# A scan in four-step blocks: how many groups of state are added over PSUM in each step, and when the next block's decays are made

## The chip, the cores and the metric

The kernel runs on one core of a Trainium2 chip. The metric is the time of one execution on the device in microseconds, as the median of several runs. A profiled execution of the same program gives the trace that the text reads; its engines are called PE (TensorE), DVE (VectorE), ACT (ScalarE), POOL (GpSimd) and SP (SyncE, which only issues DMAs here).

## The reference, cut to what matters

A small vision tower of two layers runs over 64 images of 37 tokens and 256 features. The token layer embeds patches; layer 0 has a state-space block ("attn") and a mixture of experts; layer 1 has attention and another mixture. The change lies in the scan of the state-space block:

```python
def _L0_attn_ref(up_x, ...):
    ...
    delta = jax.nn.softplus(x @ W_delta + b_delta)
    Bm = x @ W_B + b_B
    Cm = x @ W_C + b_C
    A = -jnp.exp(A_log)
    dA = jnp.exp(delta[..., None] * A)
    dBx = delta[..., None] * Bm[:, :, None, :] * x[..., None]
    def step(h, inputs):
        dA_t, dBx_t, C_t = inputs
        h = dA_t * h + dBx_t
        y_t = jnp.einsum('bdn,bn->bd', h, C_t)
        return (h, y_t)
```

There are 37 steps. The state h of one step has 64 images x 128 channels x 64 values, in float32.

## The kernel before, in words

**Layout.** Two images share the 128 partitions (64 values of n each), so the state of a step is 32 pairs x 128 channels = 4096 columns. It lies in one of eight slots of SBUF, `slot[slot_of(t)]`. The 4096 columns are four groups (GROUPS, m = 0 to 3) of 1024, and each group is two halves of 512, one PSUM bank each.

**Blocks.** Steps 1 to 36 form nine blocks of four (BLK = 4). The decays dA of a whole block are made ahead, into the four slots in which that block's states will then be formed (the decay is multiplied in place). They are made in 32 "quads" (QUADS, four channels each): `make_quad` (L1181) has PE multiply into one of three PSUM banks, `exp_quad` (L1654, its activation on L1659) has ACT take the exponential into the slots. The three banks (DECAY_BANKS, 0 to 2) are a ring that quads and the turned rows of y share; `RING_AT` gives each its place, the semaphore `made` counts the banks that PE filled, `taken` those that ACT emptied. `quads_made(t, m)` says which quads of the next block are made behind group m of step t, on PE and ACT alike: 32 quads spread evenly from group 3 of the block's first step on, so 2, 10, 10 and 10 in its four steps. ACT's first quad of a block waits until the first step of the running block has consumed the slots. DVE's first decay of a block waits for all of them (L2010).

**A step on DVE.** A group is treated in one of two ways. In the first (groups 0 and 2), DVE multiplies the slot's decay by the state before (`decay_state`, L2014), PE forms the injection dBx as two products of 512 columns in the banks 3 and 4 (`inject`, its matmuls on L1188 and L1195 by `make_quad` and `inject_rows`), and DVE adds it (`add_injected`, L2033; L2030 in step 0). In the second (groups 1 and 3, "grown"), DVE writes decay times state straight into the banks 5 and 6, half by half (`seed_state`, L2022), PE adds the injection on top of it in the bank (`grow`, matmuls on L1195), and ACT copies the sum to the slot (`copy_grown`, L1686). There is one pair of banks for each way, so each seed half waits until the copy before it has emptied its bank, and each injection until the add before it is done. The semaphores are `multed`, `injected` and `added` for the first way, `seeded`, `grown` and `copied` for the second; every wait is for a count.

**Reading.** `read_state` (L1228) multiplies half of a step's state (groups 0 and 1, or 2 and 3) by windows of C that POOL sets (L1044), eight matmuls into bank 7. ACT evicts the bank every other step (`evict_rows`, L1668), PE turns the rows (`turn_y`, L1239) into a ring bank and ACT copies y out (`copy_y`, L1678).

**The order is written out by hand.** Each engine takes its own list strictly in order. PE in step t: inject(0), the read of groups 2 and 3 of the step before, the quads behind group 0; grow(1), quads; inject(2), the read of groups 0 and 1, quads; grow(3), in odd steps turn_y, quads. ACT: quads of group 0; in odd steps evict_rows; the copies of group 1, quads; quads of group 2; the copies of group 3, in odd steps copy_y, quads. DVE: decay 0, seeds 1, add 0, decay 2, seeds 3, add 2. SP loads the injection's operands three steps ahead (`load_inject`, L891 and L892) when `injected` and `grown` tell that a buffer is free, and loads a block's delta rows when `made` allows.

Of the kernel before, what the change touches and what calls it, by code (L numbers as in the profile page):

```python
# [13 lines left out]
NI, L = 64, 37  # L14
# [86 lines left out]
def build(nc, small, dense, patches, w_lin, a_rows, up0, dn0, w1, w2, b1, b2, gates_dram, slots,  # L101
          rows_dram, delta_dram, late_rows, late_delta, h_dram, gate_dram, out):
    with ExitStack() as ctx:
# [641 lines left out]
        def quads_made(t, m):  # L745


            b = block_of(t) + 1
            if t == 0 or b >= NBLK:
                return []  # L750
            u = (t - BLK * (b - 1) - 1) * GROUPS + m - 3
            if u < 0:
                return []
            n = BLK * GROUPS - 3
            return [(b, k) for k in range(QUADS * u // n, QUADS * (u + 1) // n)]

# [25 lines left out]
        def _(sp):  # L782
# [98 lines left out]
            def load_inject(t):  # L881

                if t >= INJ:
                    sp.wait_ge(injected, 2 * (t - INJ + 1))
                    sp.wait_ge(grown, 4 * (t - INJ + 1))
                n = t % INJ
                dx_rows, b_rows = [rows_dram[w, t % 2, :, :, t // 2 * P:t // 2 * P + P].rearrange(
                    "(m p) k d -> (p k) m d", m=GROUPS) for w in range(2)]
                for x in range(8):
                    rows = slice(16 * x, 16 * x + 16)  # L890
                    sp.dma_start(dx_in[n][rows, :, x % 4, :], dx_rows[rows]).then_inc(inject_in[n], 16)  # L891
                sp.dma_start(b_in[n], b_rows).then_inc(inject_in[n], 16)  # L892
# [47 lines left out]
            sp.dma_start(hF, h_dram).then_inc(kept_back, 16)  # L940
            sp.wait_ge(multed, 2 * (L - BLK))
            sp.wait_ge(seeded, 4 * (L - BLK))
            sp.wait_ge(read_ps, 2 * (L - BLK))
# [5 lines left out]
            sp.wait_ge(read_ps, 2 * L)  # L949
            sp.wait_ge(added, 2 * L)  # L950
            sp.dma_start(up0s, up0).then_inc(ffn0_in, 16)
# [30 lines left out]
        def _(pool):  # L982
# [66 lines left out]

            pool.wait_ge(injected, 2 * L)  # L1050
            pool.wait_ge(grown, 4 * L)
            nc.gpsimd.memset(xn[:, :, T:TP], 0.0).then_inc(zeros_set, 1)
# [42 lines left out]
        def _(pe):  # L1095
# [103 lines left out]
            def inject(t, m):  # L1199

                if m == 0:
                    pe.wait_ge(inject_in[t % INJ], 16 * 9 * (t // INJ + 1))
                pe.wait_ge(added, 2 * t + m // 2)
                inject_rows(t, m, 0, INJ_BANK, True)
                inject_rows(t, m, 1, INJ_BANK + 1, True).then_inc(injected, 1)

            def grow(t, m):

                for half in range(2):
                    if t >= 1:  # L1210
                        pe.wait_ge(seeded, 4 * (t - 1) + m - 1 + half + 1)
                    elif m == 3:
                        pe.wait_ge(copied, half + 1)
                    inject_rows(t, m, half, GROW_BANK + half, t == 0).then_inc(grown, 1)

            def read_state(t, r):

                yb, tp = y_block(t)
                first = r == 0 and (tp == 0 or t == 0)
                pe.wait_ge(added, 2 * t + r + 1)  # L1220
                pe.wait_ge(copied, 4 * t + 2 * r + 2)
                pe.wait_ge(window, 4 * t + 4)
# [38 lines left out]
            for t in range(L + 1):  # L1261
                for m in range(GROUPS):
                    if 1 <= t < L and m % 2 == 0:
                        inject(t, m)
                    if 1 <= t < L and m % 2 == 1:
                        grow(t, m)
# [304 lines left out]
        def _(act):  # L1571
# [109 lines left out]
            def copy_grown(t, m):  # L1681

                for half in range(2):
                    act.wait_ge(grown, 4 * t + m - 1 + half + 1)
# [13 lines left out]
            for t in range(L + 1):  # L1698
                for m in range(GROUPS):
                    if m == 1 and t % 2 == 1:  # L1700
                        evict_rows(t // 2)
                    if 1 <= t < L and m % 2 == 1:
                        copy_grown(t, m)
                    if t < L and m == 3 and t % 2 == 1:
                        copy_y(t // 2)
                    for b, k in quads_made(t, m) if t < L else []:
                        if k == 0:
                            act.wait_ge(read_ps, 2 * (BLK * (b - 1) + 1))
                            act.wait_ge(multed, 2 * (BLK * (b - 1) + 1))
                            act.wait_ge(seeded, 4 * (BLK * (b - 1) + 1))  # L1710
# [142 lines left out]
        def _(dve):  # L1853
# [151 lines left out]
            GW = GP * P  # L2005

            def decay_state(t, m):

                if m == 0 and (t - 1) % BLK == 0:
                    dve.wait_ge(taken, block_taken(block_of(t)))  # L2010
                dve.wait_ge(added, 2 * (t - 1) + m // 2 + 1)
                now, before = slot[slot_of(t)], slot[slot_of(t - 1)]
# [3 lines left out]
            def seed_state(t, m):  # L2016

                now, before = slot[slot_of(t)], slot[slot_of(t - 1)]
                for half in range(2):
                    hs = slice((2 * m + half) * 512, (2 * m + half + 1) * 512)  # L2020
                    dve.wait_ge(copied, 4 * (t - 1) + m - 1 + 2 + half + 1)
                    nc.vector.tensor_tensor(ps[:, GROW_BANK + half, :], now[:, hs], before[:, hs],  # L2022
                                            ALU.mult).then_inc(seeded, 1)

            def add_injected(t, m):

                now = slot[slot_of(t)][:, m * GW:(m + 1) * GW].rearrange("p (b n) -> p b n", b=2)
                dve.wait_ge(injected, 2 * t + m // 2 + 1)
                if t == 0:
                    nc.vector.tensor_copy(now, ps[:, INJ_BANK:INJ_BANK + 2, :]).then_inc(added, 1)  # L2030
                else:
                    dve.wait_ge(multed, 2 * (t - 1) + m // 2 + 1)
# [376 lines left out]
```

## Time and profile before

| what | us |
|---|---|
| median of 3 runs | 1099.65 (1097.55 to 1106.23) |
| the profiled execution | 1094.59 |
| its span in the trace | 1092.7 |
| first decay of step 1 to the last read of the scan | 152.22 to 449.75 of that span |
| the rest: ahead of the scan / behind it | 152.2 / 643.0 |

Times in the rows are microseconds from the span's start, and mean durations are nanoseconds where marked. The brackets at the end of a timeline row give how long the engine was idle before it and whose instruction released it. PEclk is the granted clock of TensorE as a share of full speed: 1.0 is 2.4 GHz and 0.5 is 1.2 GHz. "L" numbers are lines of the kernel before.

### The profile page before, as it was taken

The page shows a single profiled execution, that of the slowest core. Times are in us where ns is not written, and L with a number is a line of the kernel's source. Part 1 is how long each engine was busy: PE and PEld are TensorE (multiplying, and loading weights), DVE is VectorE, ACT ScalarE, POOL GpSimd, SP SyncE. Part 2 cuts the span into 40 slices and gives each one's busy share as a digit, 9 for nine tenths or more (in the row PEclk, how much of TensorE's full clock was granted, in tenths as well). Part 3 has the DMA queues.
Part 4 walks back from the last instruction along what each step waited for, and adds up shares of the span by engine and source line. Part 5 has one row for each costly group of instructions (what it writes and reads, how often), then busy time and mean ns, then how long its engine had stood idle before and what let it go on. Part 6 is the DMA issues. An engine that isn't in the chain of part 4 may idle for free.

```text
span 1092.7 us, 17549 instructions
## 1 busy us (share of the span) xinstructions
PE 921.2 (84%) x5861; PEld 582.3 (53%) x5862; DVE 669.3 (61%) x1176; ACT 503.3 (46%) x1019; POOL 294.6 (27%) x357
## 2 busy tenths in 40 slices
PE   8997487877777777799999999999999996469996
PEld 6773443333323322346677777666667664336664
DVE  2533987988888988754554455477777773213332
ACT  1226577877779776343122222335444432323332
POOL 4922922333333310000000000074445410612222
PEclk9999768988999889999999999999999996579999
DMA  6282769453221212850411111000000002322220
GB/s 247 98 285 98 229 206 313 118 131 71 51 54 34 54 30 70 357 233 7 130 45 45 44 46 43 0 1 1 1 1 0 1 1 115 153 90 86 83 85 26
DMA packets 96258, 100.66 MB, mean 92 GB/s; under 512 B 64318, under 2 KB 81471, under 8 KB 94528
## 3 DMA queue, kind: packets, MB, share of 16 engines
q1 hardware_dynamic: 93456, 92.50, 26.7%
q0 software_dynamic: 2736, 7.30, 1.8%
q8 instruction: 39, 0.64, 0.2%
q14 instruction: 27, 0.22, 0.1%
HBM read 73.10 MB, written 39.18 MB: 103 GB/s over the span
## 4 chain that ended last, share of the span: by engine, by line
PE 64%; ACT 11%; DVE 10%; issue 7%; SPq 3%; DMA 3%; POOL 0%; ACTq 0%; DVEq 0%; POOLq 0%
PE ps L556 9%; PE ps L618 8%; PE ps L1228 6%; ACT mem L1659 5%; PE ps L1109 4%; PE ps L1518 4%; PE ps L1534 4%; PE ps L1431 3%; PE ps L1365 3%; PE ps L1188 3%; SPq L891 2%; PE ps L1387 2%; PE ps L1195 2%; ACT mem L1686 2%; DVE mem L2014 2%
## 5 line engine op out<-in xcount | busy, mean ns | idle before, releaser
L1066 POOL TENSOR_TENSOR mem<-mem,sm 128x296 f32<-128x296 f32 x128 | 87.2, 716 | 346.5 <-ACT mem L1754 306.4
L1659 ACT ACTIVATE mem<-ps 128x512 f32<-128x512 f32 x288 | 154.2, 629 | 24.0 <-PE ps L1188 12.9
L1044 POOL TENSOR_SCALAR mem<-mem,sm 128x16 f32<-128x16 f32 x148 | 105.4, 735 | 170.8 <-PE ps L1228 170.8
L556 PE MATMUL ps<-mem 128*128 (+1 forms) x384 | 110.2, 416 | 0.6 <-DVE mem L529 0.6
L1188 PE MATMUL ps<-mem 64*128 64x128 bf16 x1140 | 91.9, 232 | 20.6 <-ACT mem L1659 11.3
L1228 PE MATMUL ps<-mem 128*32 128x512 f32 x592 | 89.1, 675 | 22.3 <-issue 13.2
L1686 ACT ACTIVATE mem<-ps 128x512 f32<-128x512 f32 x148 | 82.3, 607 | 51.2 <-PE ps L1195 51.1
L1188 PEld LDWEIGHTS ps<-mem 64*128 64x128 bf16 x1140 | 56.4, 100 | 90.1 <-ACT mem L1659 69.4
L2014 DVE TENSOR_TENSOR mem<-mem 128x1024 f32<-128x1024 f32 x72 | 87.8, 1219 | 26.7 <-ACT mem L1659 26.7
L1195 PE MATMUL ps<-mem 64*128 64x512 bf16 x296 | 76.3, 424 | 31.5 <-DVE ps L2022 21.6
L2022 DVE TENSOR_TENSOR ps<-mem 128x512 f32<-128x512 f32 x144 | 93.6, 695 | 14.9 <-ACT mem L1686 14.3
L618 PE MATMUL ps<-mem 128*128 128x296 f32 x352 | 99.9, 413 | 2.5 <-DVE mem L682 2.5
L642 ACT ACTIVATE mem<-ps 128x296 f32<-128x296 f32 x88 | 36.8, 418 | 135.0 <-PE ps L556 135.0
L2033 DVE TENSOR_TENSOR mem<-mem,ps 128x1024 f32<-128x1024 f32 x72 | 87.4, 1214 | 2.1 <-PE ps L1195 1.6
L556 PEld LDWEIGHTS ps<-mem 128*128 128x128 f32 x384 | 73.1, 191 | 25.1 <-issue 2.1
L618 PEld LDWEIGHTS ps<-mem 128*128 128x128 f32 x352 | 66.6, 190 | 24.2 <-DVE mem L682 3.9
L682 DVE TENSOR_TENSOR mem<-mem 128x296 f32<-128x296 f32 x88 | 41.1, 467 | 36.5 <-ACT mem L642 34.3
L1195 PEld LDWEIGHTS ps<-mem 64*128 64x128 bf16 x296 | 21.2, 97 | 71.3 <-DVE ps L2022 54.7
L676 DVE TENSOR_TENSOR mem<-mem 128x296 f32<-128x296 f32 x64 | 29.9, 467 | 45.3 <-ACT mem L642 39.4
L1518 PE MATMUL ps<-mem 128*128 x104 | 51.1, 615 | 7.7 <-issue 7.1
L1109 PE MATMUL ps<-mem 128*128 128x288 f32 x192 | 50.7, 417 | 5.1 <-DMA mem<-in_patches 5.1
L463 DVE TENSOR_TENSOR mem<-mem 128x592 f32<-128x592 f32 (+1 forms) x32 | 26.2, 817 | 46.7 <-ACT mem L436 46.7
(240 smaller groups left out, 1573.1 us busy)
## 6 DMA issues: line engine op xcount, KB each, us to landing
mem<-gates SPq DMA_DIRECT2D x7, 1184.0 KB, 6.0
mem<-in_w SPq DMA_DIRECT2D x2, 4096.0 KB, 16.3
slots<-mem SPq DMA_DIRECT2D x1, 6682.0 KB, 23.6
mem<-slots SPq DMA_DIRECT2D x26, 257.0 KB, 2.7
mem<-in_patches SPq DMA_DIRECT2D x7, 864.0 KB, 4.7
mem<-factor_rows SPq DMA_DIRECT2D x296, 16.0 KB, 1.8
mem<-factor_rows SPq DMA_DIRECT2D x37, 128.0 KB, 2.3
mem<-delta_rows SPq DMA_DIRECT2D x9, 512.0 KB, 4.5
```

Of the source, the lines that this page charges most:

```text
L556: mm = nc.tensor.matmul(ps[:, bank, 0:CH], w[:, k, row0:row0 + P], xn[:, k, cols], start=(k == 0), stop=(k == HALVES - 1))
L618: mm = nc.tensor.matmul(ps[:, 1 + 2 * cj + m, 0:CH], dn_w[:, j - 2, m * P:(m + 1) * P], hid2[:, b, :], start=(j == 2 and n == nt), stop=(j ...
L1044: nc.gpsimd.tensor_scalar(c_win4[:, t % SLOTS * 2 + r, :, w0:w0 + 8].rearrange("p j (x i) -> p j x i", i=2)[:, :, :, i], c_all[:, r * 16:r ...
L1109: mm = nc.tensor.matmul(ps[:, 2 * j + m, 0:IC * NP], wl[:, f, m * P:(m + 1) * P], xin[:, j, f, :], start=(f == 0), stop=(f == FK - 1))
L1188: mm = nc.tensor.matmul(ps[:, ring_bank(at_), e * BT:(e + 1) * BT], a_stat[64 * r:64 * r + 64, g, e, :], delta_in[b % 2][64 * r:64 * r + 6 ...
L1195: return nc.tensor.matmul(ps[:, bank, :], b_in[t % INJ][rows, m, :], dx_in[t % INJ][rows, m, :, :].rearrange("p x n -> p (x n)"), start=st ...
L1228: mm = nc.tensor.matmul(ps[32 * j:32 * j + 32, Y_BANK, :], c_win[:, win:win + 32], slot[slot_of(t)][:, quad * 512:(quad + 1) * 512], start ...
L1518: mm = nc.tensor.matmul(ps[:, 2 + j, 0:HID1], slot_xT[j][:, k, :], w1s[:, k, ds(e * HID1, HID1)], start=(k == 0), stop=(k == 1))
L1659: nc.scalar.activation(decay_slots[b % 2][:, :, 4 * k:4 * k + 4], ps[:, ring_bank(at_), :].rearrange("p (e t) -> p t e", e=4), ACT.Exp).th ...
L1686: nc.scalar.activation(slot[slot_of(t)][:, quad * 512:(quad + 1) * 512], ps[:, GROW_BANK + half, :], ACT.Copy).then_inc(copied, 1)
L2014: nc.vector.tensor_tensor(now[:, gs], now[:, gs], before[:, gs], ALU.mult).then_inc(multed, 1)
L2022: nc.vector.tensor_tensor(ps[:, GROW_BANK + half, :], now[:, hs], before[:, hs], ALU.mult).then_inc(seeded, 1)
```

## The change

Which groups are grown now depends on the step. In step 0 they are 1 and 3 as before. In the first step of each block, and in all of the last four steps (33 to 36), they are 1, 2 and 3. In the second step of a block they are 1 and 3, in the third and fourth only group 1. Over a block that is 3, 2, 1 and 1 in place of 2, 2, 2 and 2. The next block's quads are spread anew: one behind group 3 of the first step, then 8, 11 and 12 in the second to fourth step, evenly over their groups. All waits that counted two groups a step by arithmetic now look their counts up in two tables, `ADDED_AT` and `GROWN_AT`, or count with `added_to` and `grown_to`. A seed now waits for the state of the step before in so many words (`wait_state`), as a decay does. PE's, ACT's and DVE's loops keep their order over the groups; each group is simply injected or grown as the table says.

```diff
-            u = (t - BLK * (b - 1) - 1) * GROUPS + m - 3
-            if u < 0:
-                return []
-            n = BLK * GROUPS - 3
-            return [(b, k) for k in range(QUADS * u // n, QUADS * (u + 1) // n)]
+            at_ = t - BLK * (b - 1) - 1
+            first, n = ((0, 1), (1, 8), (9, 11), (20, 12))[at_]
+            if at_ == 0:
+                return [(b, 0)] if m == 3 else []
+            return [(b, k) for k in range(first + n * m // GROUPS, first + n * (m + 1) // GROUPS)]
+
+        def grown_groups(t):
+
+            if t == 0:
+                return (1, 3)
+            if (t - 1) % BLK == 0 or t >= L - BLK:
+                return (1, 2, 3)
+            return (1, 3) if (t - 1) % BLK == 1 else (1,)
+
+        ADDED_AT, GROWN_AT = {}, {}
+        for t in range(L):
+            for m in range(GROUPS):
+                if m in grown_groups(t):
+                    GROWN_AT[t, m] = len(GROWN_AT)
+                else:
+                    ADDED_AT[t, m] = len(ADDED_AT)
+
+        def added_to(t, m=GROUPS - 1):
+
+            return len([g for g in ADDED_AT if g <= (t, m)])
+
+        def grown_to(t, m=GROUPS - 1):
+
+            return len([g for g in GROWN_AT if g <= (t, m)])
...
-                    sp.wait_ge(injected, 2 * (t - INJ + 1))
-                    sp.wait_ge(grown, 4 * (t - INJ + 1))
+                    sp.wait_ge(injected, added_to(t - INJ))
+                    sp.wait_ge(grown, 2 * grown_to(t - INJ))
...
-                pe.wait_ge(added, 2 * t + m // 2)
+                pe.wait_ge(added, ADDED_AT[t, m])
...
-                        pe.wait_ge(seeded, 4 * (t - 1) + m - 1 + half + 1)
+                        pe.wait_ge(seeded, 2 * GROWN_AT[t, m] - 4 + half + 1)
...
-                pe.wait_ge(added, 2 * t + r + 1)
-                pe.wait_ge(copied, 4 * t + 2 * r + 2)
+                pe.wait_ge(added, added_to(t, 2 * r + 1))
+                pe.wait_ge(copied, 2 * grown_to(t, 2 * r + 1))
...
-                    if 1 <= t < L and m % 2 == 0:
+                    if 1 <= t < L and (t, m) in ADDED_AT:
                         inject(t, m)
-                    if 1 <= t < L and m % 2 == 1:
+                    if 1 <= t < L and (t, m) in GROWN_AT:
                         grow(t, m)
...
+            def wait_state(t, m):
+
+                if m in grown_groups(t):
+                    dve.wait_ge(copied, 2 * GROWN_AT[t, m] + 2)
+                else:
+                    dve.wait_ge(added, ADDED_AT[t, m] + 1)
...
             for t in range(L):
-                for m in range(0, GROUPS, 2):
-                    if t >= 1:
-                        decay_state(t, m)
-                        seed_state(t, m + 1)
-                    add_injected(t, m)
+                for m in range(GROUPS):
+                    by_pe = grown_groups(t)
+                    if m not in by_pe:
+                        if t >= 1:
+                            decay_state(t, m)
+                        if t >= 1 and m + 1 in by_pe:
+                            seed_state(t, m + 1)
+                        add_injected(t, m)
+                    elif t >= 1 and m - 1 in by_pe:
+                        seed_state(t, m)
```

So DVE's order in a step with three grown groups is decay 0, seeds 1, add 0, seeds 2, seeds 3, and with one: decay 0, seeds 1, add 0, decay 2, add 2, decay 3, add 3. The same replacement of counts is made in ACT's, POOL's and SP's other waits.

## Rows read from the trace of the kernel before

**Rows 1.** The page: span, busy time and share of each engine
```profile
span 1092.7 us, 17549 instructions
...
PE 921.2 (84%) x5861; PEld 582.3 (53%) x5862; DVE 669.3 (61%) x1176; ACT 503.3 (46%) x1019; POOL 294.6 (27%) x357
```
**Rows 2.** Windows by block: stretch, length, busy by engine, PEclk, DMA share, GB/s
```profile
152.22:188.76 36.54, 29.05 (x258) 11.53 (x250) 28.43 (x32) 26.78 (x55) 8.72 (x17) 0.86 0.96 306
188.76:221.66 32.90, 25.14 (x240) 10.56 (x240) 28.42 (x33) 26.06 (x53) 12.06 (x17) 0.90 0.48 125
221.66:255.09 33.43, 25.51 (x240) 11.00 (x240) 28.51 (x32) 26.04 (x53) 12.04 (x17) 0.90 0.49 126
...
288.82:321.20 32.38, 24.20 (x240) 10.03 (x240) 28.31 (x33) 26.05 (x53) 9.99 (x17) 0.95 0.23 51
...
421.84:449.75 27.91, 18.78 (x103) 5.26 (x103) 27.85 (x32) 11.03 (x20) 0.20 (x1) 0.94 0.58 219
```
**Rows 3.** Waits between 222 and 421 us (total, times, longest)
```profile
ACT mem L1686 <- PE ps L1195: 30.1, 14, 3.2
DVE mem L2014 <- ACT mem L1659: 18.8, 6, 3.1
...
DVE ps L2022 <- ACT mem L1686: 9.2, 17, 0.7
```
**Rows 4.** Timeline from the head of the block of steps 9 to 12
```profile
221.66 1.23 DVE L2014 TENSOR_TENSOR mem<-mem 128x1024 f32<-128x1024 f32 x1 [3.13 <-ACT mem L1659]
222.80 1.31 DVE L2022 TENSOR_TENSOR ps<-mem 128x512 f32<-128x512 f32 x2
...
223.55 0.43 PE L1195 MATMUL ps<-mem 64*128 64x512 bf16 x1 [2.23 <-DVE ps L2022]
224.01 0.60 ACT L1686 ACTIVATE mem<-ps 128x512 f32<-128x512 f32 x1 [1.90 <-PE ps L1195]
224.02 1.21 DVE L2033 TENSOR_TENSOR mem<-mem,ps 128x1024 f32<-128x1024 f32 x1
...
225.15 1.21 DVE L2014 TENSOR_TENSOR mem<-mem 128x1024 f32<-128x1024 f32 x1
...
225.83 1.93 PE L1228 MATMUL ps<-mem 128*32 128x512 f32 x8
226.29 1.29 DVE L2022 TENSOR_TENSOR ps<-mem 128x512 f32<-128x512 f32 x2
...
227.69 0.61 PE L1195 MATMUL ps<-mem 64*128 64x512 bf16 x2
...
228.23 2.08 PE L1239 MATMUL ps<-sm,mem 128*128 128x128 f32 x8
...
230.53 0.14 PEld L1195 LDWEIGHTS ps<-mem 64*128 64x128 bf16 x2
...
233.34 1.09 ACT L1686 ACTIVATE mem<-ps 128x512 f32<-128x512 f32 x2
```
**Rows 5.** Timeline in other steps: turn, y copy, exponentials, products and a read
```profile
210.32 1.16 PE L1239 MATMUL ps<-sm,mem 128*128 128x128 f32 x8
...
212.12 0.35 ACT L1678 ACTIVATE mem<-ps 128x128 f32<-128x128 f32 x1
212.29 1.62 ACT L1659 ACTIVATE mem<-ps 128x512 f32<-128x512 f32 x3
...
290.71 0.39 PE L1195 MATMUL ps<-mem 64*128 64x512 bf16 x1 [2.23 <-DVE ps L2022]
...
297.05 1.06 PE L1228 MATMUL ps<-mem 128*32 128x512 f32 x8
```
**Rows 6.** Timeline of the first block: two waits that a DMA ended
```profile
162.35 2.06 ACT L1659 ACTIVATE mem<-ps 128x512 f32<-128x512 f32 x4 [2.16 <-DMA late_rows<-mem]
...
178.90 0.39 PE L1195 MATMUL ps<-mem 64*128 64x512 bf16 x2 [0.69 <-DMA mem<-factor_rows]
```
**Rows 7.** Timeline: the last read of the scan
```profile
449.75 1.07 PE L1228 MATMUL ps<-mem 128*32 128x512 f32 x8 [0.73 <-DVE mem L2033]
```

More of the change, by code:

```diff
@@ L940, in _ @@
             sp.dma_start(hF, h_dram).then_inc(kept_back, 16)
-            sp.wait_ge(multed, 2 * (L - BLK))
-            sp.wait_ge(seeded, 4 * (L - BLK))
+            sp.wait_ge(multed, added_to(L - BLK) - 2)
+            sp.wait_ge(seeded, 2 * grown_to(L - BLK) - 4)
             sp.wait_ge(read_ps, 2 * (L - BLK))
@@ L949, in _ @@
             sp.wait_ge(read_ps, 2 * L)
-            sp.wait_ge(added, 2 * L)
+            sp.wait_ge(added, added_to(L - 1))
             sp.dma_start(up0s, up0).then_inc(ffn0_in, 16)
@@ L1048, in _ @@
                             S("c_half")[:, i:i + 1], None, ALU.mult).then_inc(window, 1)
-            pool.wait_ge(injected, 2 * L)
-            pool.wait_ge(grown, 4 * L)
+            pool.wait_ge(injected, added_to(L - 1))
+            pool.wait_ge(grown, 2 * grown_to(L - 1))
             nc.gpsimd.memset(xn[:, :, T:TP], 0.0).then_inc(zeros_set, 1)
@@ L1683, in copy_grown @@
                 for half in range(2):
-                    act.wait_ge(grown, 4 * t + m - 1 + half + 1)
+                    act.wait_ge(grown, 2 * GROWN_AT[t, m] + half + 1)
                     quad = 2 * m + half
@@ L1701, in _ @@
                         evict_rows(t // 2)
-                    if 1 <= t < L and m % 2 == 1:
+                    if 1 <= t < L and (t, m) in GROWN_AT:
                         copy_grown(t, m)
@@ L1708, in _ @@
                             act.wait_ge(read_ps, 2 * (BLK * (b - 1) + 1))
-                            act.wait_ge(multed, 2 * (BLK * (b - 1) + 1))
-                            act.wait_ge(seeded, 4 * (BLK * (b - 1) + 1))
+                            act.wait_ge(multed, added_to(BLK * (b - 1) + 1) - 2)
+                            act.wait_ge(seeded, 2 * grown_to(BLK * (b - 1) + 1) - 4)
                             if b == 1:
@@ L2010, in decay_state @@
                     dve.wait_ge(taken, block_taken(block_of(t)))
-                dve.wait_ge(added, 2 * (t - 1) + m // 2 + 1)
+                wait_state(t - 1, m)
                 now, before = slot[slot_of(t)], slot[slot_of(t - 1)]
@@ L2016, in seed_state @@
             def seed_state(t, m):
+                wait_state(t - 1, m)
                 now, before = slot[slot_of(t)], slot[slot_of(t - 1)]
@@ L2020, in seed_state @@
                     hs = slice((2 * m + half) * 512, (2 * m + half + 1) * 512)
-                    dve.wait_ge(copied, 4 * (t - 1) + m - 1 + 2 + half + 1)
+                    dve.wait_ge(copied, 2 * GROWN_AT[t, m] - 2 + half + 1)
                     nc.vector.tensor_tensor(ps[:, GROW_BANK + half, :], now[:, hs], before[:, hs],
@@ L2027, in add_injected @@
                 now = slot[slot_of(t)][:, m * GW:(m + 1) * GW].rearrange("p (b n) -> p b n", b=2)
-                dve.wait_ge(injected, 2 * t + m // 2 + 1)
+                dve.wait_ge(injected, ADDED_AT[t, m] + 1)
                 if t == 0:
@@ L2031, in add_injected @@
                 else:
-                    dve.wait_ge(multed, 2 * (t - 1) + m // 2 + 1)
+                    dve.wait_ge(multed, ADDED_AT[t, m] - 2 + 1)
                     nc.vector.tensor_tensor(now, now, ps[:, INJ_BANK:INJ_BANK + 2, :], ALU.add).then_inc(added, 1)
             for t in range(L):
-                for m in range(0, GROUPS, 2):
-                    if t >= 1:
-                        decay_state(t, m)
-                        seed_state(t, m + 1)
-                    add_injected(t, m)
+                for m in range(GROUPS):
[8 more added lines that the diff above has]
+                        seed_state(t, m)
             dve.wait_ge(kept_back, 16 * 4)
```

## The prediction

> **What bounds the kernel now.** The page comes first: a span of 1092.7 us, TensorE (PE) busy for 84% of it, VectorE (DVE) for 61%, ScalarE (ACT) for 46% [rows 1]. Those shares average over stages, and the edit lies in one of them, so the view that counts is the table of windows with one row for each block of four steps [rows 2]. There DVE is busy 28.4 to 28.5 us of some 33 and ACT 26.05. Neither is full, and both have nearly as much to do as the block is long. From T = 188.76 (first decay of the block of steps 5 to 8) to T = 421.84 lie seven blocks, 33.30 us each. The first takes 36.54 with the DMA rings at 0.96, and the last, which makes no decays, 27.91. The waits tell what the missing 5 us are: DVE's largest is for the exponentials, 3.1 us ahead of each block (18.8 us in six blocks), then 9.2 us for ACT's copies ahead of seeds. ACT in turn waits 30.1 us for the products of grown groups, 14 times [rows 3]. So a block begins with ACT waiting for DVE and ends with DVE waiting for ACT: a load that is uneven in time, which is what the edit addresses.
>
> **Unit costs.** In one block [rows 4]: decay at 221.66, its seed pair at 222.80, the add at 224.02, the next decay at 225.15. So DVE issues a decay every 1.13 us, a seed pair takes 1.21, an add 1.13. A group with decay and add costs 2.26, a grown one 1.21; a step of two and two 6.94. ACT issues a copy or exponential every 0.49 (a pair takes 1.09, one 0.60); after a y copy it is free in 0.17 (212.12 to 212.29) [rows 4, 5]. A seed half runs 0.69, its product starts 0.06 later and takes 0.39 to 0.43, the copy starts at once and takes 0.60: 1.85 us from the seed's start until its bank is free.
>
> **The change, counted.** Grown groups go from 2,2,2,2 to 3,2,1,1 in the four steps of a block. DVE: 5.89 + 6.94 + 7.99 + 7.99 = 28.8 us for 27.8 before. ACT: 14 copies for 16, 1.0 us less. Decays still take 32 exponentials, now 1, 8, 11, 12 for 2, 10, 10, 10. The products number the same on PE. The renumbered waits on SP and POOL ask for the same events, so their queues aren't moved past anything: 0. The added wait ahead of a seed asks for the state of the step before, which the bank wait behind it or DVE's own order had already: 0; only seeds and adds are queued behind it. Totals hardly change, so the time depends on the chain. I follow it in two parts, cut at c, the end of the copies of group 1 in the block's second step.
>
> *From T to c.* Before: 221.66 to 233.34 + 1.09 = 234.43, 12.77 us [rows 4]. Its chain was seed of group 3 at T+4.63, read of the state (1.93), product at T+6.03, the turn of y (2.08), the first decays, injection at T+8.87, read, decays, product, copy [rows 4]. Now group 3's seed needs the banks that group 2 has just taken: group 1 seeded at 1.13, add 2.35, group 2 seeded at 3.49, its copies end at 5.26 and 5.87, group 3 seeded at 5.31 and 5.92, DVE free at 6.52 (0.42 earlier than 6.94, not the counted 1.05). On PE the read sits between the products of groups 2 and 3. With a read at 1.06 and a turn at 1.16 [rows 5]: read 5.1 to 6.1, product 6.1 and 6.67, turn from 6.95, quad 8.04, injection 8.25, read 8.6, two quads 9.6 to 10.05, their exponentials until 10.88, copies until 11.97. The read and the turn are at their slow lengths in most blocks of before, though, and these now lie in series behind a product that comes later: 0.9 more for a slow read and 0.9 for a slow turn. Slow read alone: c = 12.4 to 12.9; both: 13.3 to 13.7. I take 12.75, nearest to the row of before, 12.77.
>
> *From c to the next T.* Before: 255.09 - 234.43 = 20.66 [rows 2, 4], in which ACT has 28 exponentials, 10 copies, an eviction and a y copy: 38 x 0.49 + 0.66 = 19.3, and 1.4 of gaps. Now 29 exponentials, 6 copies and the same two: 35 x 0.49 + 0.66 = 17.8. The gaps grow, since with two quads made a turn ACT runs out while PE reads: after the copies it is busy 0.87, the next quad comes 1.30 after them. That is 0.43 twice in the second step, 0.44 ahead of the turn in the third, and 0.54 behind a read at the start of the fourth: 1.85 in all, so 19.7. DVE in the same part: 0.65 of waiting for the third injection of the third step, and at the end it waits 1.1 instead of 3.1, since group 3 of the last step is no longer a copy in front of the last exponentials.
>
> Block: 12.75 + 19.7 = 32.45 for 33.43, 0.97 less. Seven of them: -6.8 us. The first block has waits for DMA in it (0.69 at an injection, 2.16 at an exponential [rows 6]) that a faster step would only lengthen: -0.5, between -1.5 and 0.
>
> *The last four steps* have three grown groups each and no decays. Before, DVE paces them, 27.91 us from T to the last read [rows 2, 7]. The count promises 4 x 1.05 = 4.2 less. But the round trip of 1.85 through one pair of banks three times a step, with the read between, and two turns of y, brings the last read to T+28.1 by the same hand working, since that read now waits for a copy (0.5 behind the seed's product) and no longer for an add. With a slow clock there, 29. I take +0.5; ends -4.2 and +1.1.
>
> **Sum.** -6.8 - 0.5 + 0.5 = -6.8 us. The profiled execution took 1094.59 (1.9 around its span of 1092.7) and becomes 1087.8. The median of the runs shown lies 5.1 higher, 1099.65, and takes the same difference: 1092.9, say 1093.
>
> **The clock.** The blocks' granted clock is 0.90 (0.95 in one), that is 6.7 us (3.2 us) of each at 1.2 GHz [rows 2]. It shows after PE had stood idle for 2.23 us and then in short gaps: products of 0.61 in place of 0.39, reads of 1.93 in place of 1.06 [rows 4, 5]. The block with 0.95 is the shortest, 32.38. In the changed kernel the idle stretch at the block's head is about as poor in work: between T+0.4 and T+5.1 only the four products of groups 1 and 2, in gaps of 1.5, 0.2 and 1.3 us.
>
> The Trainium skill (TensorE: Matmul & The Clock Gate, "A second HAM failure mode: psum-queue depth-cycling") says that a kernel which cycles PSUM in each iteration leaves micro-idles between groups of matmuls that make the clock swing between its two levels. The trace agrees for the idle of 2.23 us; no row shows three groups in a row through one bank pair, and by this rule they would be what the last rival below prices.
>
> **Rivals.**
> (A) The forecast, 1093, chance 0.46; its own range 1089 to 1096.
> (B) The clock stays high at most block heads, as it does in the last steps of before. For: the 3.13 us wait that opened the gap is gone. Against: the gaps just listed. T to c is 12.0, so 1.6 to 1.75 less for each of seven blocks, -1.5 in the first: about -13, 1086. Chance 0.18.
> (C) DVE's count alone decides, the gaps of ACT close up: 6.52 + 6.94 + 7.99 + 7.99 + 0.6 for the last exponentials = 30.0 a block, 3.3 less: -23, 1077. For: ACT's counted work, 48 x 0.49 and two y copies, is 24 us. Against: quads come in threes through three banks, and ACT had such gaps before too. Chance 0.10.
> (D) The gain of the second part is lost in the first: c at 13.3 to 13.7 in most blocks, within 2 us of no change, 1099. For: the late product of group 3. Chance 0.16.
> (E) Slower. Place: the first step of each block, where three seeds go through one pair of banks. If the clock falls later than before and still is low at the turn of y and at the read behind it, each doubles: injection at T+10.5, read until 12.4, c at 15.0, so 2.2 more in the first part against 0.97 less in the second: +1.25 in eight blocks, +2 in the last steps, +12: 1112. It decides from c = T+13.75 on. Chance 0.10.
> That the edit doesn't do what it says is no case: orders and counts follow from the code.
>
> **From these to the numbers.** A measurement here can tell about 1% (11 us) from no change. Faster by over 1% (under 1088.7): C, nearly all of B, a little of A: 0.28. Slower by over 1%: 0.08, most of E. Within 1%: 0.64. For 8 in 10 the range leaves out C, most of E: 1081 to 1103.
>
> **What would show it.** Right: windows of the seven blocks at 32.4 on average; DVE's wait for exponentials at each head 0.9 to 1.5 in place of 3.1; seed pairs of groups 2 and 3 that take 1.3, 0.6 apart; c at T+12 to 13; exponentials ahead of c three, not four; the last read 28 to 29 after the last T. Wrong: a wait at the head over 2 us; c to T' over 20.3; an injection that DVE waits for in every step (PE's order would be the bound); last steps under 26. The forecast falls if the granted clock of the scan leaves 0.90 by more than 0.04.

## The result, and the profile after

The changed kernel is slower: a median of 1113.73 us (1111.8 to 1116.13, 4 runs) against 1098.75 (4 runs), a ratio of 1.0119 with a 95% interval of 1.0089 to 1.015. Forecast were 1093, in a range from 1081 to 1103.

The profiled execution has a span of 1114.2 us, 21.5 more than before. First the windows by block, the same view as [rows 2] (stretch, length, busy time by engine, PEclk, DMA share, GB/s), and the parts ahead of and behind the scan:

```profile
0.00:155.89 155.89, 126.62 (x648) 90.91 (x649) 78.08 (x114) 67.32 (x126) 81.43 (x67) 0.87 0.53 182
...
155.89:191.88 35.99, 29.57 (x258) 11.61 (x250) 29.84 (x32) 26.35 (x52) 8.28 (x16) 0.84 0.99 304
191.88:226.35 34.47, 26.46 (x244) 11.24 (x240) 29.76 (x32) 25.63 (x50) 9.77 (x16) 0.90 0.48 127
...
363.31:397.45 34.14, 26.35 (x244) 11.04 (x240) 29.75 (x32) 25.63 (x50) 9.76 (x16) 0.90 0.22 47
...
431.59:464.86 33.27, 23.64 (x107) 6.86 (x104) 24.65 (x32) 15.36 (x28) 0.21 (x1) 0.74 0.49 185
464.86:1114.20 649.34, 582.41 (x3181) 406.74 (x3181) 333.28 (x774) 215.32 (x456) 131.20 (x173) 0.93 0.18 60
```

and the two outer parts of the kernel before:

```profile
0.00:152.22 152.22, 122.35 (x648) 88.25 (x649) 80.06 (x115) 67.28 (x126) 81.19 (x67) 0.89 0.54 186
...
449.75:1092.70 642.95, 573.89 (x3181) 401.74 (x3181) 333.72 (x774) 215.86 (x456) 131.24 (x173) 0.94 0.18 61
```

The 21.5 us split into +3.7 ahead of the scan and +6.4 behind it, in code that isn't changed, and +11.4 in the scan. Of these the first block gives -0.55, the seven blocks +6.6 (34.24 us each in place of 33.30), the last four steps +5.4 (33.27 in place of 27.91). The counts of work came out about as forecast: DVE is busy 29.75 in a block for 28.5 (1.0 more was counted), ACT 25.63 for 26.05 (1.0 less was counted, 0.4 came). Neither explains a block that is 0.94 longer. The time is in the chain. One execution stands behind each of these rows, and the blocks' part of the difference isn't fixed to better than some 2 us: the run e4 below has the same code in its seven blocks, and there they took 33.94 each.

The timeline from the head of the last block that makes decays, T = 397.45, answers to [rows 4]:

```profile
397.45 1.23 DVE L2045 TENSOR_TENSOR mem<-mem 128x1024 f32<-128x1024 f32 x1 [1.14 <-ACT mem L1683]
...
400.94 1.29 DVE L2054 TENSOR_TENSOR ps<-mem 128x512 f32<-128x512 f32 x2
401.69 1.21 PE L1219 MATMUL ps<-mem 64*128 64x512 bf16 x2 [1.13 <-DVE ps L2054]
402.33 1.20 ACT L1710 ACTIVATE mem<-ps 128x512 f32<-128x512 f32 x2 [1.14 <-PE ps L1219]
402.82 1.93 PE L1252 MATMUL ps<-mem 128*32 128x512 f32 x8
403.03 1.30 DVE L2054 TENSOR_TENSOR ps<-mem 128x512 f32<-128x512 f32 x2 [0.80 <-ACT mem L1710]
...
404.69 0.61 PE L1219 MATMUL ps<-mem 64*128 64x512 bf16 x2
405.23 1.78 PE L1263 MATMUL ps<-sm,mem 128*128 128x128 f32 x8
...
409.88 1.09 ACT L1710 ACTIVATE mem<-ps 128x512 f32<-128x512 f32 x2
```

The wait at the head has shrunk as forecast, from 3.13 to 1.14. Group 3's seeds start at T+5.58 with 0.80 of waiting for group 2's copy; its product starts at T+7.24, behind a read of 1.93 at the low clock; before, it started at T+6.03. The copies of group 1 in the second step end at c = 410.97 = T+13.52. From there to the next T it is 20.62 us, in each of the seven blocks, where it was 20.66. So the second part saved 0.04, and the first lost 1.0 (13.63 on average over the seven blocks, 12.64 before).

### The profile page after: what moved, and what is told of

It is laid out like the page before. It is cut to its first block, busy times and chain, and to the rows that moved or that the text cites. A ratio compares the mean times of both kernels' runs of the same rounds, so it can differ in the third digit from the quotient of the medians.

```text
span 1114.2 us, 17613 instructions
## 1 busy us (share of the span) xinstructions
PE 947.0 (85%) x5861; PEld 593.9 (53%) x5862; DVE 674.1 (61%) x1176; ACT 503.8 (45%) x1011; POOL 282.4 (25%) x357
## 4 chain that ended last, share of the span: by engine, by line
PE 68%; ACT 10%; DVE 10%; issue 9%; DMA 2%; POOL 0%; ACTq 0%; DVEq 0%; SPq 0%; POOLq 0%
PE ps L556 8%; PE ps L618 8%; PE ps L1252 7%; ACT mem L1683 5%; PE ps L1133 4%; PE ps L1542 4%; PE ps L1558 4%; PE ps L1455 3%; PE ps L1219 3%; PE ps L1389 3%; PE ps L1212 3%; PE ps L1263 2%; PE ps L1411 2%; DVE ps L2054 2%; PE ps L1401 2%
## 5 line engine op out<-in xcount | busy, mean ns | idle before, releaser
L1683 ACT ACTIVATE mem<-ps 128x512 f32<-128x512 f32 x288 | 153.1, 624 | 29.2 <-PE ps L1212 20.5
L1068 POOL TENSOR_SCALAR mem<-mem,sm 128x16 f32<-128x16 f32 x148 | 93.0, 651 | 189.2 <-PE ps L1252 189.2
L1219 PE MATMUL ps<-mem 64*128 64x512 bf16 x296 | 85.4, 429 | 31.2 <-DVE ps L2054 29.8
L2054 DVE TENSOR_TENSOR ps<-mem 128x512 f32<-128x512 f32 x136 | 88.4, 695 | 23.3 <-ACT mem L1710 23.0
L1212 PEld LDWEIGHTS ps<-mem 64*128 64x128 bf16 x1140 | 56.8, 98 | 83.8 <-ACT mem L1683 73.7
L1710 ACT ACTIVATE mem<-ps 128x512 f32<-128x512 f32 x140 | 78.8, 607 | 48.5 <-PE ps L1219 48.4
L2065 DVE TENSOR_TENSOR mem<-mem,ps 128x1024 f32<-128x1024 f32 x76 | 92.5, 1218 | 11.6 <-PE ps L1219 8.7
L2045 DVE TENSOR_TENSOR mem<-mem 128x1024 f32<-128x1024 f32 x76 | 92.7, 1220 | 10.9 <-ACT mem L1683 10.9
L1219 PEld LDWEIGHTS ps<-mem 64*128 64x128 bf16 x296 | 23.3, 96 | 78.9 <-DVE ps L2054 72.0
```

The costliest lines, as they stand in the source:

```text
L1068: nc.gpsimd.tensor_scalar(c_win4[:, t % SLOTS * 2 + r, :, w0:w0 + 8].rearrange("p j (x i) -> p j x i", i=2)[:, :, :, i], c_all[:, r * 16:r ...
L1212: mm = nc.tensor.matmul(ps[:, ring_bank(at_), e * BT:(e + 1) * BT], a_stat[64 * r:64 * r + 64, g, e, :], delta_in[b % 2][64 * r:64 * r + 6 ...
L1219: return nc.tensor.matmul(ps[:, bank, :], b_in[t % INJ][rows, m, :], dx_in[t % INJ][rows, m, :, :].rearrange("p x n -> p (x n)"), start=st ...
L1683: nc.scalar.activation(decay_slots[b % 2][:, :, 4 * k:4 * k + 4], ps[:, ring_bank(at_), :].rearrange("p (e t) -> p t e", e=4), ACT.Exp).th ...
L2045: nc.vector.tensor_tensor(now[:, gs], now[:, gs], before[:, gs], ALU.mult).then_inc(multed, 1)
```

## The experiments

Two theories were set against each other, and a third beside them. Clock: the head is lengthened by products, a read and a turn of y at the low clock. Round trip: three groups through one bank pair cost at any clock. Late quads: 12 quads in the fourth step are the loss. The three don't exclude each other, and the loss has several places, so each run is read by stage. Below, "first part" is T to c and "second part" c to the next T. All ratios are to the kernel before, run on the same chip.

**e1_warm_after and e2_warm_before: idle products at the heads.**

```diff
+            def fill(t, n, head=True):
...
+                at_ = RING_AT["y", t // 2]
+                pe.wait_ge(taken, at_ - DECAY_BANKS + 1)
+                for _ in range(n):
+                    nc.tensor.matmul(ps[:, ring_bank(at_), :], b_in[t % INJ][:, 0, :],
...
...
+                    if t < L and m < 2:
+                        fill(t, 6 if m == 0 else 4)
```

A test at the start of `fill`, not shown here, lets it run only in a block's first step and in the last four steps. In e2 the counts are 9 and 3.

> The changed kernel with products that nobody reads (6 behind the read at the head of each block's first step and of the last four steps, 4 behind group 1), written to a free ring bank, so that PE does not stand idle there. Clock theory: the granted clock stays at 1.0 through the heads; from a block's first decay to the end of the copies of group 1 in its second step 12.0 us in place of 13.5, blocks 32.7 in place of 34.2, the last four steps 28 to 29 in place of 33.3; in all 15 to 17 us less than the changed kernel, near the kernel before or 1 to 4 us under it. Round-trip theory (one bank pair for three groups costs at any clock): less than 4 us gained. Late-quads theory: nothing gained.

> The kernel before with the same idle products (9 and 3 a head). Clock theory: its heads also pay, 12.8 to about 11.2 us up to the copies in the second step, blocks 31.7 in place of 33.3, nothing in the last four steps (DVE paces them): 10 to 13 us less, a ratio of 0.988 to 0.991. Round-trip and late-quads theories: no statement; the time stays if the low clock is hidden behind DVE.

Measured: e1 1101.45 us, ratio 1.0014 (0.9986 to 1.0042); e2 1092.31, ratio 0.994 (0.9916 to 0.9963). A later block of e1, the end of its first part, and its last four steps; then the same of e2, with one more of its blocks:

```profile
322.64:355.42 32.78, 26.75 (x254) 11.24 (x250) 29.59 (x33) 25.71 (x50) 9.16 (x16) 1.00 0.23 50
333.71 1.09 ACT L1723 ACTIVATE mem<-ps 128x512 f32<-128x512 f32 x2
420.95:453.65 32.70, 27.60 (x146) 8.60 (x143) 24.28 (x32) 15.72 (x28) 0.20 (x1) 1.00 0.50 188
```

```profile
253.46:285.55 32.09, 26.37 (x253) 11.20 (x252) 28.24 (x32) 26.15 (x53) 9.10 (x17) 1.00 0.23 50
263.80 1.09 ACT L1699 ACTIVATE mem<-ps 128x512 f32<-128x512 f32 x2
317.64:350.77 33.13, 27.93 (x253) 11.70 (x252) 28.25 (x32) 26.21 (x53) 9.10 (x17) 0.95 0.22 49
414.96:444.56 29.60, 26.16 (x149) 8.66 (x148) 28.13 (x32) 10.58 (x20) 0.20 (x1) 1.00 0.54 206
```

At a granted clock of 1.00 the first part is 12.16 in e1 (13.52 to 13.85 without) and 11.43 in e2 (11.7 to 13.2). The second part stays at 20.62 and 20.66, since there the clock was full in the kernels without idle products too. A low clock costs there too: in e2's block from 317.64 on it fell in the second part, to one half from 336.95 to 340.36, a read took 1.89, DVE then waited 1.07 for a copy, and the part is 21.70, 1.04 longer. So the low clock took 1.4 to 1.7 us a block from the changed kernel and 1.2 from the kernel before, whose heads I had not counted as paying. That parts the loss of 1.0 in the first part: at the full clock the two kernels are 0.73 apart (12.16 and 11.43), which is the new order of the work, and only some 0.3 is what the low clock takes more from the new order than from the old one.

The last four steps did not come out as the clock theory said: 32.70 at clock 1.00, and in e2 the idle products even lengthened them from 27.91 to 29.60. There they stand in the way. In all, e1 is 11.6 us below the changed kernel by the ratios, for 15 to 17 expected, more than the round-trip theory's 4. e2 is 6.6 below the kernel before, for 10 to 13 expected: its blocks are 32.24 on average and not 31.7, and the last steps took 1.7 of the gain back.

**e3_split_only, e5_groups_only: each half of the change by itself.**

```diff
e3, on the kernel before:
-            u = (t - BLK * (b - 1) - 1) * GROUPS + m - 3
...
+            first, n = ((0, 1), (1, 8), (9, 11), (20, 12))[at_]
...
e5, on the changed kernel: the same lines the other way round
```

> The kernel before with only the quads spread anew (1, 8, 11, 12). Clock theory and round-trip theory: about as before, within 3 us, since the head's chain keeps its order; one quad less at the head may give 0.3 a block. Late-quads theory: the whole loss of the blocks, 0.9 each, 6 to 8 us slower.

Measured: 1107.44 us, ratio 1.0062 (1.0034 to 1.0091). The clock and round-trip theories had said no change within 3 us; it is what the late-quads theory says (6.8 us slower by the ratio, for 6 to 8). The second part grew from 20.66 to 22.13, within 0.01 in all seven blocks. The block, the end of its first part, and the head behind it, whose wait grew from 3.13 to 3.62:

```profile
363.45:397.61 34.16, 25.13 (x240) 10.69 (x240) 28.34 (x33) 26.04 (x53) 11.11 (x17) 0.95 0.22 47
374.38 1.09 ACT L1686 ACTIVATE mem<-ps 128x512 f32<-128x512 f32 x2
```

```profile
397.61 1.23 DVE L2014 TENSOR_TENSOR mem<-mem 128x1024 f32<-128x1024 f32 x1 [3.62 <-ACT mem L1659]
```

The chain of the changed kernel from 410 us on shows why (start, duration, what; merged, in order of time):

```profile
411.07 1.07 PE ps L1252 x8
412.14 0.34 PE ps L1212 x8
412.48 0.02 issue
412.50 0.61 ACT mem L1683
...
413.77 0.90 issue
414.67 1.07 PE ps L1252 x8
```

It is a loop of 3.60 us a half step: a read, 0.34 to make two quads behind it, two exponentials, two copies, then the next read, which waits for the copies (the "issue" of 0.90 is ACT's two copies: ACT L1710 at 413.48, 1.10 long). Before, the loop has the same 3.6 (reads at 230.94 and 234.53) with two and three quads in turn: the third stands behind an odd group, PE makes it ahead of the read, and ACT takes its exponential while PE reads. So taking quads from ten to eight in the second step saved nothing, while a third quad behind group 2 in the third step, and behind groups 0 and 2 in the fourth, costs 0.49 each, three times.

> The changed kernel with the quads spread as before (2, 10, 10, 10), groups 3, 2, 1, 1. Loop theory (in the second part of a block PE and ACT take turns: read, two quads behind it, their exponentials, two copies, 3.6 us a half step however many quads stand behind the odd group, so that eight quads save nothing in the second step and three behind groups 0 and 2 cost 0.49 each in the fourth): from the copies in the second step to the next block 20.6 - 1.5 = 19.1 us, the first part 0.4 longer than 13.5 since one quad more is made ahead of c; blocks 33.0, 1.1 less than the changed kernel, ratio 1.003 to 1.007. Rival (the new spread is what balances ACT): slower than the changed kernel, the second part over 20.6.

Measured: 1107.27 us, ratio 1.0051 (1.0032 to 1.007); the second part is 19.04 to 19.05 in all seven blocks, as the loop theory has it (here 388.20 less the end of the copies at 369.16). The first part is 13.2 to 15.2, 14.3 on average for 13.9 expected, with a granted clock down to 0.85, so blocks average 33.37 where 33.0 were expected.

```profile
355.52:388.20 32.68, 25.44 (x240) 11.17 (x240) 29.62 (x33) 25.74 (x50) 9.01 (x16) 0.95 0.22 49
368.07 1.09 ACT L1710 ACTIVATE mem<-ps 128x512 f32<-128x512 f32 x2
```

**e4_last_as_before, e6_last_only, e7_two_pairs: the last four steps.**

```diff
e4: groups 1 and 3 in steps 33 to 36, all else as changed
e6: groups 1, 2 and 3 in steps 33 to 36, all else as before
e7, on the changed kernel:
+        def pair_of(m):
+            return INJ_BANK if m == 2 else GROW_BANK
...
-                    dve.wait_ge(copied, 2 * GROWN_AT[t, m] - 2 + half + 1)
+                    if m == 2:
+                        dve.wait_ge(added, ADDED_AT[t, 0] + 1)
+                    elif m == 3 and 2 in grown_groups(t):
+                        dve.wait_ge(copied, 2 * GROWN_AT[t, m] - 4 + half + 1)
+                    else:
...
+                if m == 0 and 2 in grown_groups(t - 1):
+                    pe.wait_ge(copied, 2 * GROWN_AT[t - 1, 2] + 2)
```

> The changed kernel with groups 1 and 3 grown in the last four steps, as before. All theories: these steps go back from 33.3 to about 28 us, 5 us less than the changed kernel. What differs is what is left: clock and round-trip theories leave 6 us over the kernel before in the blocks, a ratio of 1.005 to 1.008.

> The kernel before with three grown groups only in the last four steps. Round-trip theory: those steps take 33 us in place of 27.9, all blocks as before (33.3 on average), ratio 1.004 to 1.006. Clock theory (the low clock in them came from the blocks ahead, which had settled on one phase): 29 to 30 us.

> The changed kernel with group 2's seeds, products and copies in the injection's pair of banks (3 and 4), free from the add of group 0 to the next step's injection. Round-trip theory: the waits of 0.8 ahead of the seeds of groups 2 and 3 go, the last four steps fall from 33.3 to 28 to 29, blocks lose 0 to 0.7; 5 to 9 us less than the changed kernel. Clock theory: PE's order (the read between two products) and the low clock set the head, so blocks stay at 34.1 and the last four steps at 31 or more; under 3 us.

Measured: e4 1104.08 us, ratio 1.0046 (1.0026 to 1.0066); e6 1105.93, 1.0041 (1.0014 to 1.0068); e7 1106.45, 1.0053 (1.0027 to 1.0079). The last four steps of e4, e6 and e7 in that order:

```profile
425.62:454.85 29.23, 21.72 (x106) 6.65 (x103) 27.95 (x32) 10.83 (x20) 0.20 (x1) 0.77 0.56 210
```

```profile
420.92:455.76 34.84, 24.25 (x102) 6.83 (x103) 24.93 (x32) 15.14 (x28) 0.20 (x1) 0.69 0.46 175
```

```profile
434.05:463.45 29.40, 20.36 (x107) 5.83 (x103) 24.24 (x32) 15.29 (x28) 0.20 (x1) 0.83 0.55 209
```

e6 takes the blocks out of the question: its seven are those of before to 0.06 us, and three grown groups alone lengthen the last four steps by 6.9. e7 gives group 2 its own bank pair and gets 3.9 of the changed kernel's 5.4 back, while its blocks stay at 34.2 to 35.1 with a first part of 13.5 and more: there the clock and PE's order decide, not the banks. By the ratio e7 is 7 us below the changed kernel, which looks like the round-trip theory's 5 to 9, but over the whole scan its profiled execution is only 0.8 shorter (308.2 us for 309.0), so the windows support 3.9 in the last steps and nothing in the blocks. e4 goes back to 29.23, not quite to 27.91: at a clock of 0.77 the copies of its last group end 0.6 behind the last add, and the last read waits for them. Both theories hold, each in its place. In the last steps the granted clock also falls, to 0.74 and 0.69. Two runs bound its share. At a clock of 1.00 e1 still took 32.70 for 33.27, and its idle products may stand in the way as e2's did, by 1.7; so my estimate of the clock's share of the 5.4 is 0.6 to 2.3, the rest being the round trips. No run separates the two further.

**e10_read_behind: the read that lies between the products.**

```diff
-                    if t < L and m == 2:
+                    if t < L and m == (3 if 2 in grown_groups(t) else 2):
                         read_state(t, 0)
```

> The changed kernel with the read of groups 0 and 1 moved behind group 3's product in steps with three grown groups. If the read between the products is what delays group 3 (product now at T+7.2), product and copies come 0.5 to 0.9 earlier, but the read then stands between it and the turn of y, so T to c stays within 0.3 of 13.5 or grows by up to 1; the last four steps fall by 1 to 3 us. If the bank's round trip is what delays it, the product comes less than 0.3 earlier and the last steps stay within 1 us.

Measured: 1133.81 us, ratio 1.031 (1.0262 to 1.0359). Group 3's product starts at T+6.33, 0.9 earlier, as the first case has it, but the first part grows to 14.9 to 16.4, more than expected, and the last four steps rise to 38.29 in place of falling. The first line is DVE's first add in a block's second step, the next one its counterpart in the changed kernel:

```profile
421.50 1.22 DVE L2065 TENSOR_TENSOR mem<-mem,ps 128x1024 f32<-128x1024 f32 x1 [2.49 <-PE ps L1219]
```

```profile
407.60 1.22 DVE L2065 TENSOR_TENSOR mem<-mem,ps 128x1024 f32<-128x1024 f32 x1 [0.27 <-PE ps L1219]
```

```profile
445.49:483.78 38.29, 26.75 (x98) 7.13 (x94) 24.57 (x32) 15.03 (x27) 0.00 (x0) 0.66 0.42 161
```

Both of these blocks have a granted clock of 0.90. The read is better where it delays the product, since PE is idle in that gap. What decides the first part is when PE reaches the next step's injection, for which DVE waits 2.49 here and 0.27 in the changed kernel, not when group 3 is copied. In four of the seven blocks the clock was lower still (0.86), and these are the longest, 15.8 to 16.4.

**e8_two_fewer, e11_one_fewer, e9_warm_two_fewer, e12_warm_groups: what of the change is worth keeping.**

```diff
         def grown_groups(t):
e8, e9: return (1,) if (t - 1) % BLK >= 2 and t < L - BLK else (1, 3)
e11:    return (1,) if (t - 1) % BLK == 3 and t < L - BLK else (1, 3)
all four: quads 2, 10, 10, 10 as before; e9 and e12 with idle products at the heads, e12 with groups 3, 2, 1, 1
```

> Groups 1 and 3 grown in the first two steps of a block and in the last four, only group 1 in the third and fourth (2, 2, 1, 1), quads as before. The head is that of the kernel before, the second part that of the run with the old spread. Loop theory: first part 12.8, second 19.1, blocks 31.9 (1.4 under the kernel before), last four steps 27.9: 10 to 12 us less than before, ratio 0.989 to 0.992. If the blocks settle on the clock's phase as the changed kernel's did, less is gained: 0.995 to 1.

> Groups 2, 2, 2, 1 with the quads as before: only the block's fourth step is changed. DVE's own count is 6.94 x 3 + 8.3 = 29.1. Loop theory: one pair of copies fewer ahead of the block's last exponentials takes the 3.1 us wait at the head down to 2 or less, second part 19.6 to 19.9, blocks 31.5 to 32.3, ratio 0.987 to 0.993. If the whole gain of 2, 2, 1, 1 comes from the last step's copies alone, it is 0.983 here too.

> Groups 2, 2, 1, 1 with the quads as before, plus 6 and 3 idle products at the heads of the eight blocks that make decays. In the run without them DVE is never idle from the fifth block on (30.70 us each), and the first part is 11.4 to 12.7. Clock theory: only the earlier blocks gain, 0.3 to 1.0 each, 2 to 4 us in all; the later ones stay at 30.7 since DVE paces them. Rival (the clock still holds the later blocks back): these fall below 30.3.

> Groups 3, 2, 1, 1, quads as before, with 6 and 4 idle products at the heads of the eight blocks that make decays. Clock theory: first part 12.6 (12.16 with the new spread, one exponential more), second 19.05, blocks 31.6; the last four steps near 33. If the third grown group at the head were a gain at a full clock, blocks would be under the 30.7 of 2, 2, 1, 1.

Measured: e8 1082.3 us, ratio 0.9829 (0.9803 to 0.9856), faster than both kernels; e11 1089.29, 0.9905 (0.9875 to 0.9934); e9 1084.19, 0.9839 (0.9772 to 0.9907); e12 1099.35, 1.0002 (0.9974 to 1.003). Two later blocks and the last steps of e8:

```profile
344.84:375.55 30.71, 24.62 (x240) 10.12 (x240) 30.29 (x34) 24.39 (x48) 7.70 (x16) 0.94 0.24 53
375.55:406.25 30.70, 24.61 (x240) 10.12 (x240) 30.28 (x34) 24.39 (x48) 3.22 (x4) 0.94 0.16 35
406.25:434.14 27.89, 20.17 (x112) 5.50 (x112) 27.84 (x33) 11.09 (x20) 0.20 (x1) 0.94 0.59 221
```

DVE has taken over as the bound: 30.28 us of work in 30.70. e8 did better than expected (30.99 a block on average for 31.9): the head's wait for exponentials is gone in the later blocks, and the first part with it falls to 11.44. In e11 the second part is 19.68, inside its expectation (20.70 in the one block in which the clock fell there), with blocks of 31.4 to 34.7 (32.4 on average, a little over it); of the 1.6 us that e8's second part gains, the fourth step's pair of copies gives 1.0. e9 misses: idle products held the clock up in two blocks only (1.00 and 0.99, 30.69 and 30.67 us), the others had 0.90 to 0.95 and took up to 33.05, so nothing was gained over e8 in the median; one of its four runs took 1072.91, at a granted clock of 0.94 over the whole execution for 0.93 in the others, and isn't explained. e12's blocks were 31.74 at a clock of 1.00, as expected, and 33.3 to 33.4 in those with 0.95; even the full clock leaves the third grown group at the head 1.0 behind e8:

```profile
317.69:351.07 33.38, 27.52 (x250) 11.13 (x250) 29.65 (x33) 25.60 (x50) 8.02 (x16) 0.95 0.22 49
351.07:382.81 31.74, 25.88 (x250) 10.91 (x250) 29.64 (x33) 25.60 (x50) 8.37 (x16) 1.00 0.23 51
```

The second parts side by side (us, from the starts of decays and the ends of copies in each trace):

| groups grown | quads 2, 10, 10, 10 | quads 1, 8, 11, 12 |
|---|---|---|
| 2, 2, 2, 2 | 20.66 (before, e2, e6) | 22.13 (e3) |
| 2, 2, 2, 1 | 19.68 (e11) | |
| 2, 2, 1, 1 | 19.04 to 19.27 (e8) | |
| 3, 2, 1, 1 | 19.05 (e5, e12) | 20.62 (changed, e1, e4, e7, e10) |

Blocks in which the clock fell in the second part are left out (one of e2, one of e11), and so is e9, whose second parts are 19.07 to 20.61.

Fewer copies save 1.6 and the new spread of quads gives back 1.6 (1.5 with the old groups, in e3). The third group at the head costs 1.3 in the first part at the full clock and with the same quads (12.70 in e12, 11.43 in e2, whose idle products differ a little in number), of which the new spread, with one quad less there, gives back 0.5 (12.16 in e1). With the 0.3 that the low clock takes more, this comes to the 0.94 by which the blocks grew.

## Why the prediction was wrong

- **What bounds the kernel: right.** ACT waits for DVE at a block's head and DVE for ACT at its end, and the head's wait fell to 1.14, within the 0.9 to 1.5 forecast.
- **Counts: right but for one term.** DVE's step with one grown group is 8.4, not 7.99: an add that stands straight behind its own group's decay, for which it waits, is issued 1.32 after it (342.38 and 343.70 in e8), not 1.13. This is hidden in the changed kernel, and is part of what bounds e8.
- **From T to c: the step that failed first.** I took 12.75, between the full clock (11.97, 12.16 measured in e1) and both read and turn slow (13.3 to 13.7). The changed kernel took 13.52 to 13.85 in all seven blocks. The chain was right, and the two prices nearly (0.9 each; the clock took 1.4 to 1.7 in all). The choice of the middle, "nearest to the row of before", was not: the row of before, 12.77, holds a slow read and a slow turn already, and at the full clock it is 11.43. The new order had to be added to it, 0.73 by e1 and e2, because the read now waits on PE behind group 2's products, which need DVE's seeds, where it stood behind an injection that needed only an add (they start at T+4.24 and T+3.63). The clock was down for 0.10 x 2 x 34.14 = 6.8 us of each block, as in most blocks before. +0.9 a block against the term used.
- **From c to the next T: the second.** I forecast 19.7 and the trace has 20.62, past the 20.3 that was to show the forecast wrong. I had the first exponential behind a read 1.30 after the copies; in the trace they end at 410.97 and it starts at 412.50, 1.53 after, and such a gap recurs at each read. The larger fault is in the reading: I counted ACT's operations and gaps, and did not see that the loop of 3.6 a half step doesn't shorten when quads are taken out of it. The trace of before has reads 3.6 apart there, and I did not ask what sets that distance. +0.9 a block.
- **The last four steps: the third.** I took +0.5 within -4.2 and +1.1; measured +5.4, outside both ends. The hand working put the last read at T+28.1 at the full clock; e1 needed 32.70 there, with idle products that cost up to 1.7. So it is the round trips that were under-priced, by 3.9 (e7 against the changed kernel). The clock, 0.94 before, fell to 0.74; I had allowed 0.9 for that; the estimate from e1 and e2 is 0.6 to 2.3.
- **The first block:** -0.5 forecast, -0.55 measured. That is luck: e6 has the kernel before's code there and took 37.01 for 36.54.
- **The sum.** The gain of 0.97 was also taken from one block of 33.43, where the mean of the seven is 33.30, so the working really gave 0.85 a block. Together: seven times 0.88 in the first part, seven times 0.92 in the second, 4.9 in the last steps and 0.9 for the wrong base make the 18.2 us between -6.8 and +11.4.
- **The rivals.** D and E together are what happened: D's place and its c (13.3 to 13.7), E's sign and nearly its size in the result, 1113.7 for 1112. But E's mechanism asked for c past T+13.75, which only the first of the seven blocks reached (13.85); the scan's loss beyond D is the second part that saved nothing and the last steps, and some 10 us of the profiled difference lie outside the scan. That the time came so near to E's is luck. B's condition (a high clock) was made in e1, and gave 12.16 for 12.0. The count of DVE (C) is no bound in the changed kernel.
- **The clock page.** The Trainium skill (TensorE: Matmul & The Clock Gate, "A second HAM failure mode: psum-queue depth-cycling") says that short idle stretches between groups of matmuls, in a kernel that cycles through PSUM in each iteration, make the clock swing between its two levels. The trace of the last four steps agrees that it swings: the granted clock went from 0.94 to 0.74 with three groups through one bank pair, and with two pairs it was 0.83. That the bank pair is the reason is not shown: with groups 1 and 3 alone the same steps had 0.88 in e3 and 0.77 in e4.

**What stays open.** The scan accounts for 11.4 of the 15.0 us between the medians (13 by the ratio). The rest lies in unchanged code: the 3181 matmuls behind the scan took 582.41 us of PE time at a granted clock of 0.93, before 573.89 at 0.94, and over the profiles of all these kernels that part ranges from 640.5 (e4) to 650.1 us (e5) with no order that follows an edit. Whether the changed scan has a part in it was not tried.

## What to carry to other kernels

Counts of work per engine say which engine could be the bound, not what a rebalancing gives: find the loop that two engines run in turn, and ask of each item moved whether it lies in that loop or beside it. Here a quad beside the read was free, one behind it cost 0.49 us, and a copy ahead of the last exponentials cost all of itself. Of a change in three parts, take each alone: the part that relieved the third and fourth steps was worth 1.7% (e8), and the other two, the new spread and the third group (at the heads and in the last steps), spent more than that. Where a chain passes through TensorE behind an idle stretch, price it at the low clock unless the trace shows otherwise, and price the kernel before in the same way: compare low with low and full with full.

## What the runs showed of the hardware

A stretch at the low clock costs by where it falls. In the first part of a block it took 1.4 to 1.7 us from the changed kernel; in the second part it took 1.04 in e2 (21.70 for 20.66) and 1.02 in e11 (20.70 for 19.68); in the last four steps, which DVE paces when two groups are grown, 27.91 us were reached at 0.94 (before) and at 0.88 (e3), and 29.23 at 0.77 (e4).

On DVE an add that waits for the decay straight before it is issued 1.32 us after it, and one that doesn't 1.13: 0.19 for the wait (e8).

The length of a block drew towards one value in kernels with different orders. In the changed kernel it went 34.47, 34.35, 34.25, 34.19, 34.17, 34.14, 34.14; in e3 35.01, 34.63, 34.40 and down to 34.14; in e7 from 35.08 to 34.15; in e4 it rose, from 33.52 to 34.12. Their second parts are constant and differ (20.62 and 22.13), so it is the first part, the one in which the clock fell, that adjusted: in e3 from 12.88 to 12.01, in e4 from 12.91 to 13.51. A time so alike in different kernels looks like a lock on when the clock is changed. If it is one, a small saving inside such a block can vanish; that cause is argued and not shown. Where the clock was held at 1.00, blocks kept their own lengths (32.77 in e1, 32.09 in e2). In e8 they fell to 30.70, and there DVE was full. In the kernel before (32.4 to 33.8) and in e5, e6, e9, e10, e11 and e12 they did not settle.
